# Feed-forward of a six-layer block: its input fetched by DMA, its first products in three passes of a rounded format

## The chip, the cores and the metric

The kernel runs on one core of a Trainium2 chip. The core has a matrix engine (TensorE, PE in the rows; its weight loads are PEld), a vector engine (DVE), a scalar engine (ACT), GpSimd (POOL) and a queue that issues DMAs (SP). They run their own instruction lists and wait for each other on semaphores. The metric is the device time of one execution in microseconds; lower is better.

## The reference

The input `x` is 16 sequences of 128 tokens of 128 features. It goes through four stages, each added to `x`: a 16-head cross attention, a mixture of 16 experts, a latent cross attention with rotation, and then the stage that takes most of the time, six layers of

```
for i in range(DEPTH):                     # DEPTH = 6
    x = attn_layer(shift_tokens(x), Wqkv[i], ...) + x
    x = ffn_layer(shift_tokens(x), ln_g[i], ln_b[i], W1[i], b1[i], W2[i], b2[i]) + x

def shift_tokens(t):                       # second half of the features comes from the token before
    a, s = jnp.split(t, 2, -1)
    s = jnp.pad(s, ((0, 0), (1, 0), (0, 0)))[:, :-1]
    return jnp.concatenate([a, s], -1)

def ffn_layer(x, g, bln, W1, b1, W2, b2):
    xn = layer_norm(x) * g + bln
    a, gate = jnp.split(xn @ W1 + b1, 2, -1)   # W1 is 128 x 682
    return a * gelu(gate) @ W2 + b2            # W2 is 341 x 128
```

`attn_layer` is a windowed attention of 16 heads of 64. All is float32.

## The kernel before

Tokens stand on the 128 partitions. `Y` [128, 16, 128] holds the state of the six layers, one 128x128 tile for each of 16 sequences (b).

**Attention.** A sequence has four units of work (four heads each), so a layer has 64 units. Each engine runs a `Pipeline`: in slot c it does its steps for unit c minus the step's skew. So in one slot PE does, in this order, `l_scores` (unit c-5), `l_turn_qk` (c-4), `l_pv` (c-6), the projections (c-1), `l_output` (c-7), `l_turn_o` (c-6), `l_turn` (c-5) and `l_turn_x` (c). DVE does `l_peaks` (c-5), `l_sum_squares` (c-2), `l_divide` (c-6), `l_floor`, `l_residual`, `l_rotate` (c-1). POOL does `l_norm` (c-4: four small instructions, lines 541 to 548), `l_add` (c-3, line 534) and `l_scale` (c-4, line 555). The last slots of a layer, 64 to 70, are written `att.finish(0)` to `att.finish(6)`; in them only the units that are left are served. Note the skews: POOL's `l_add` of unit 63 needs only DVE's `l_rotate` of slot 64.

`l_pv` of the units of a sequence reads copies of the values in `stash` (`l_v2`, `l_v3`), which SP's queue makes by DMA: `move_values(b, q)` issues four DMAs of 65 KB once the values are there, and `l_pv` of unit 4b waits for all four of (b, 0). SP also fetches the shifted attention input of each sequence into `xin` with two DMAs (lines 367 and 368), of 128 rows and, for the shifted half of the features, of 127 rows.

**Feed-forward.** It runs in four groups g of four sequences, each with three chunks k of the hidden width (128, 128, 85). For a group: `f_shift` (PE, lines 923 and 924: two float32 products with an identity and a shifted identity put the shifted input into PSUM), `f_stats` (DVE, lines 1653 and 1658), the reciprocal root (POOL, lines 566 and 568), `f_norm` (DVE, line 1666), `f_turn` (PE, line 932: four transposes), `f_copy_n` (ACT, line 1227, to `f_nT`), then for each chunk `f_hidden` (PE, lines 948 and 949: two float32 products of 512 columns, each printed as two matmuls), `f_gelu` (ACT), `f_gated` (DVE), and `f_out` (PE, line 959) and `f_residual` (DVE). `f_hidden` of chunk i waits for `f_gated` of chunk i-2 (the banks alternate).

The first part is woven into the last slots: `into_feed_forward` puts steps between `att.finish(...)` calls, in an order written out by hand for each engine. The rest is in `out_of_feed_forward`, which also starts the next layer's attention and splits its weights (ACT `high_weights`, DVE `low_weights`). The attention's projections already use the format that the change brings to `f_hidden`: the operands are rounded to F32R ("high"), the remainder is kept as a second F32R tensor ("low"), and three passes high·high, high·low, low·high are added up in PSUM (lines 818 and 827).

## Time and profile before

| | us |
|---|---|
| median of 3 runs | 2300.74 (2296.83 to 2302.52) |
| the profiled execution, device time | 2298.88 |
| its span | 2297.1 |
| PE busy | 2163.7 (94%) |
| DVE busy | 1708.3 (74%) |
| ACT busy | 1555.0 (68%) |
| POOL busy | 1410.4 (61%) |
| chain that ended last: PE's share | 74% |

The profile is of one execution. The span runs from the first to the last instruction; the device time holds 1.8 us more. The six layers fill the stretch from about 560 us to the end, 288.6 us each.

### The profile page before, as it was taken

The page shows a single profiled execution, that of the slowest core. Times are in us where ns is not written, and L with a number is a line of the kernel's source. Part 1 is how long each engine was busy: PE and PEld are TensorE (multiplying, and loading weights), DVE is VectorE, ACT ScalarE, POOL GpSimd, SP SyncE. Part 2 cuts the span into 40 slices and gives each one's busy share as a digit, 9 for nine tenths or more (in the row PEclk, how much of TensorE's full clock was granted, in tenths as well). Part 3 has the DMA queues.
Part 4 walks back from the last instruction along what each step waited for, and adds up shares of the span by engine and source line. Part 5 has one row for each costly group of instructions (what it writes and reads, how often), then busy time and mean ns, then how long its engine had stood idle before and what let it go on. Part 6 is the DMA issues. An engine that isn't in the chain of part 4 may idle for free.

```text
span 2297.1 us, 104869 instructions
## 1 busy us (share of the span) xinstructions
PE 2163.7 (94%) x36357; PEld 1677.6 (73%) x36357; DVE 1708.3 (74%) x4617; ACT 1555.0 (68%) x5192; POOL 1410.4 (61%) x2639
## 2 busy tenths in 40 slices
PE   6999789998999989999899998999989999899998
PEld 4776267776888758887588875788857888578885
DVE  4777878886888758787578875778757877578874
ACT  3553545554888748887488884888848888478883
POOL 3442711112888728887288882888828888288881
PEclk9997999997999999999999999999999999999999
DMA  3000000001211102111021110311103111021110
GB/s 102 0 0 1 0 1 0 0 0 54 75 41 42 35 26 75 40 42 35 23 77 42 41 36 18 81 42 39 39 18 79 42 40 40 16 51 43 42 40 20
DMA packets 120016, 82.33 MB, mean 36 GB/s; under 512 B 50998, under 2 KB 112580, under 8 KB 119876
## 3 DMA queue, kind: packets, MB, share of 16 engines
q1 hardware_dynamic: 119876, 80.43, 13.5%
q8 instruction: 92, 1.51, 0.3%
q14 instruction: 48, 0.39, 0.1%
HBM read 21.94 MB, written 1.05 MB: 10 GB/s over the span
## 4 chain that ended last, share of the span: by engine, by line
PE 74%; issue 5%; DVE 4%; POOL 2%; ACT 1%; DVEq 0%; POOLq 0%; ACTq 0%
PE bank L818 14%; PE bank L835 9%; PE bank L902 7%; PE bank L882 6%; PE bank L862 6%; PE bank L827 6%; PE bank L892 4%; PE bank L845 4%; PE bank L757 2%; PE bank L854 2%; PE bank L746 2%; PE bank L949 2%; PE bank L948 2%; PE bank L605 2%; PE bank L959 1%
## 5 line engine op out<-in xcount | busy, mean ns | idle before, releaser
L534 POOL TENSOR_TENSOR l_qk<-l_rot 128x512 f32<-128x512 f32 x384 | 494.2, 1287 | 106.0 <-DVE l_rot L1597 58.8
L1593 DVE TENSOR_TENSOR l_rot<-bank,l_tab 128x512 f32<-128x512 f32 x384 | 265.0, 690 | 185.7 <-ACT l_sq L1194 185.1
L1210 ACT ACTIVATE l_qkT<-bank 128x512 f32<-128x512 f32 x384 | 229.6, 598 | 255.2 <-PE bank L835 255.2
L555 POOL TENSOR_TENSOR l_qk<-l_qk,l_rn 128x512 f32<-128x512 f32 x384 | 400.7, 1044 | 0.9
L1174 ACT ACTIVATE prob<-bank,peak 128x64 f32<-128x64 f32 x1536 | 353.9, 321 | 1.3 <-DVE peak L1615 1.3
L818 PE MATMUL bank<-w_high,xs_part 128*128 128x512 f32 x768 | 347.4, 452 | 6.0 <-DVE xs_part L1584 5.4
L1597 DVE TENSOR_TENSOR l_rot<-bank,l_tab 128x512 f32<-128x512 f32 x384 | 261.4, 681 | 0.0
L1607 DVE TENSOR_REDUCE l_ss<-l_sq 128x8 f32<-128x512 f32 x384 | 259.6, 676 | 0.2
L835 PE MATMUL bank<-const,l_qk 128*128 128x128 f32 x1536 | 252.9, 287 | 6.5 <-POOL l_qk L555 5.8
L1194 ACT ACTIVATE l_sq<-bank 128x512 f32<-128x512 f32 x384 | 236.0, 615 | 23.8 <-PE bank L818 16.0
L902 PE MATMUL bank<-l_wo,l_oT 128*128 128x128 f32 x1536 | 237.4, 277 | 0.0
L827 PE MATMUL bank<-w_high,xs_part 128*128 128x256 f32 x768 | 199.9, 283 | 11.6 <-issue 11.6
L902 PEld LDWEIGHTS bank<-l_wo,l_oT 128*128 128x128 f32 x1536 | 204.8, 191 | 3.3 <-issue 0.3
L835 PEld LDWEIGHTS bank<-const,l_qk 128*128 128x128 f32 x1536 | 161.9, 141 | 42.9 <-POOL l_qk L555 9.6
L818 PEld LDWEIGHTS bank<-w_high,xs_part 128*128 128x128 f32 x768 | 144.9, 189 | 63.9 <-DVE xs_part L1584 7.1
L882 PE MATMUL bank<-l_v,probT 64*32 64x65 f32 x4608 | 177.2, 223 | 10.0 <-ACT probT L1182 6.5
L439 POOL TENSOR_SCALAR ln_rs<-ln_mv 128x1 f32<-128x1 f32 (+1 forms) x64 | 14.5, 227 | 274.2 <-DVE ln_mv L1561 129.4
L1615 DVE TENSOR_REDUCE peak<-bank 128x4 f32<-128x256 f32 x384 | 160.0, 417 | 28.9 <-PE bank L862 27.3
L862 PE MATMUL bank<-l_qkT 64*32 64x64 f32 x12288 | 174.7, 222 | 0.0
L882 PEld LDWEIGHTS bank<-l_v,probT 64*32 64x32 f32 x4608 | 115.4, 106 | 79.1 <-issue 79.1
L1632 DVE TENSOR_TENSOR o<-bank,rsum 128x256 f32<-128x256 f32 x384 | 163.0, 424 | 13.3
L882 PE MATMUL bank<-stash,probT 64*32 64x65 f32 x7680 | 172.2, 223 | 0.0
(201 smaller groups left out, 5287.8 us busy)
## 6 DMA issues: line engine op xcount, KB each, us to landing
stash<-l_v SPq DMA_DIRECT2D x768, 65.0 KB, 2.0
early<-in_L_ffn_Wqkv_dram SPq DMA_DIRECT2D x36, 256.0 KB, 3.1
l_wo<-in_L_ffn_Wo_dram SPq DMA_DIRECT2D x6, 512.0 KB, 4.0
xin<-Y SPq DMA_DIRECT2D x96, 32.0 KB
xin<-Y SPq DMA_DIRECT2D x96, 31.8 KB
f_w<-in_L_ffn_W_dram SPq DMA_DIRECT2D x6, 341.0 KB
out_dram<-X SPq DMA_DIRECT2D x4, 256.0 KB, 2.3
f_w<-in_L_ffn_W_dram SPq DMA_DIRECT2D x6, 128.0 KB
```

The lines of the kernel that those rows point to most:

```text
L534: pool.tensor_tensor(l_qk[:, k], l_rot[:, k, 0], l_rot[:, k, 1], ALU.add).then_inc(l["add_done"], 1)
L555: pool.tensor_tensor(v, v, l_rn[:, k, :, None].broadcast_to([128, 8, L_DIM]), ALU.mult).then_inc(l["qk_done"], 1)
L818: ins = pe.matmul(bank[:, 0, :].rearrange("p (q n) -> p q n", q=2), xs_part[:, part, j // 4], w[:, 0:2, 256 * g:256 * g + 256], start=n == ...
L827: ins = pe.matmul(bank[:, 1, 0:256], xs_part[:, part, j // 4], w[:, 2, 256 * g:256 * g + 256], start=n == 0, stop=n == 2)
L835: ins = pe.transpose(bank[:, 2, n * 128:(n + 1) * 128], l_qk[:, j % 2, n * 128:(n + 1) * 128], ident)
L862: ins = pe.matmul(bank[w * WINDOW:(w + 1) * WINDOW, 3 + r, BAND * p:BAND * (p + 1)], l_qkT[rows, j % 2, queries:queries + WINDOW], l_qkT[r ...
L882: ins = pe.matmul(bank[w * WINDOW:(w + 1) * WINDOW, 6 - p, at:at + L_DIM + 1], probT[rows, j % 2, 128 * r + w * WINDOW:128 * r + (w + 1) * ...
L902: ins = pe.matmul(bank[:, 7, 256:384], l_oT[:, j // 4, p], l_wo[:, p], start=p == 0, stop=p == 7, skip_group_check=True)
L1174: ins = act.activation(prob[:, k, n * BAND:(n + 1) * BAND], bank[:, 3 + r, p * BAND:(p + 1) * BAND], ACT.Exp, bias=peak[:, k, n:n + 1])
L1593: dve.tensor_tensor(l_rot[:, k, 0].rearrange("p (q h n) -> p q h n", q=2, h=4), bank[:, 0, :].rearrange("p (q h n) -> p q h n", q=2, h=4), ...
L1597: dve.tensor_tensor(l_rot[:, k, 1].rearrange("p (q h s n) -> p q h s n", q=2, h=4, s=2), bank[:, 0, :].rearrange("p (q h s n) -> p q h s n ...
L1607: dve.tensor_reduce(l_ss[:, k, :, 0], l_sq[:].rearrange("p (h n) -> p h n", n=L_DIM), AX.X, ALU.add)\
```

## The change

Three things change in the six layers.

1. The shifted input of the feed-forward no longer comes from PE. SP copies it from `Y` to `f_x` (the memory of `m_xT`, free by then) with `take_feed_forward`: three groups at once behind the loop of `move_values`, when twelve sequences have their residual, and the last group when all have. DVE's statistics and normalisation read `f_x`, after a wait on the new semaphores `ld_fx`, and so does POOL before it adds `f_b2` to `Y`. `f_shift` is gone, and row 0 of the shifted half is set to zero once by POOL.
2. `f_hidden` does three F32R passes for each of its two products. For that ACT rounds `f_w1` to `f_wh` and each group's `f_nT` to `f_high`, and DVE makes the remainders `f_wl` and `f_low`.
3. Statistics, roots, normalisation and transposes are placed earlier and two groups apart, so `f_n`, `f_mv` and `f_rs` are doubled and the transposes alternate between banks 1 and 2.

The diff, cut; of the three `into_feed_forward` in it the first is POOL's, the second PE's, the third DVE's, and the `out_of_feed_forward` is DVE's.

```
+            def take_feed_forward(ly, first, end):
+                sp.wait_ge(l["res_done"], upto(ly * B, end))
+                apart(sp)
+                for b in range(first, end, 4):
+                    four = slice(b, b + 4)
+                    sp.dma_start(f_x[:, four, 0:HALF], Y[:, four, 0:HALF]).then_inc(ld_fx[b // 12], 16)
+                    sp.dma_start(f_x[1:, four, HALF:], Y[0:S - 1, four, HALF:]).then_inc(ld_fx[b // 12], 16)
...
+                take_feed_forward(ly, 0, 12)
                 for b in range(B - 2, B):
                     for q in range(2):
                         move_values(ly, b, b % 2, q)
+                take_feed_forward(ly, 12, 16)
...
+            pool.memset(f_x[0:1, :, HALF:], 0.0).then_inc(preset, 1)
...
             def into_feed_forward(ly, att):
+                rstd_n, bias = feed_forward(ly)
                 att.steady()
-                att.finish(0, 1, 2, 3)
+                att.finish(0)
+                rstd_n(0)
+                att.finish(1)
+                rstd_n(1)
+                att.finish(2, 3)
                 pool.wait_ge(ld_fw, (ly + 1) * (16 * FW_DMAS))
-                feed_forward(ly, 0)
+                bias(0)
...
-                    pe.matmul(bank[0:n, at, :], f_w1[:, FF + c0:FF + c0 + n], f_nT[:, g % 2], start=True, stop=True)
-                    pe.matmul(bank[0:n, at + 1, :], f_w1[:, c0:c0 + n], f_nT[:, g % 2], start=True, stop=True)\
-                      .then_inc(f["hidden"], 1)
+                    passes = (f_wh, f_high[:, g % 2]), (f_wl, f_high[:, g % 2]), (f_wh, f_low[g % 2])
+                    for half, first in ((0, FF + c0), (1, c0)):
+                        for m, (w, x) in enumerate(passes):
+                            ins = pe.matmul(bank[0:n, at + half, :], w[:, first:first + n], x, start=m == 0,
+                                            stop=m == 2)
+                    ins.then_inc(f["hidden"], 1)
...
             def into_feed_forward(ly, att):
-                att.finish(0, 1)
-                shift(0)
-                att.finish(2, 3)
+                att.finish(0, 1, 2)
+                turn_n(0)
+                att.finish(3)
+                turn_n(1)
                 pe.wait_ge(ld_fw, (ly + 1) * (16 * FW_DMAS))
-                turn_n(0)
                 att.finish(4)
                 hidden(0, 0)
-                att.finish(5)
-                shift(1)
-                att.finish(6)
+                att.finish(5, 6)
                 hidden(0, 1)
...
+                    act.activation(f_high[:, g % 2], f_nT[:, g % 2], ACT.Copy).then_inc(f["high_done"], 1)
...
+                act.activation(f_wh, f_w1[:], ACT.Copy).then_inc(f["wh_done"], 1)
...
             def into_feed_forward(ly, att):
-                att.finish(0, 1)
+                att.finish(0)
                 stats(0)
-                att.finish(2, 3)
+                att.finish(1)
+                stats(1)
                 norm(0)
+                att.finish(2)
+                norm(1)
+                dve.wait_ge(f["wh_done"], upto(0, ly + 1))
+                dve.tensor_tensor(f_wl, f_w1[:], f_wh.bitcast(F32), ALU.subtract).then_inc(f["w_split"], 1)
+                att.finish(3)
+                split(0)
                 att.finish(4, 5)
-                dve.wait_ge(ld_fw, (ly + 1) * (16 * FW_DMAS))
+                split(1)
                 gated(0, 0)
-                stats(1)
                 att.finish(6)
-                norm(1)
...
             def out_of_feed_forward(ly, nxt):
-                    if 0 < g < 3:
-                        stats(g + 1)
+                    if g < 2:
+                        stats(g + 2)
                     if g > 0:
                         gated(g, 0)
                     if 0 < g < 3:
-                        norm(g + 1)
+                        split(g + 1)
+                    if g < 2:
+                        norm(g + 2)
```

POOL, the last slots of the first layer, the kernel before: after the loop's branch come slot 64 (`finish(0)`: units 60, 61, 60) and slot 65. The row on `l_rn` ends `l_norm`, `l_qk<-l_rot` is `l_add`, `l_qk<-l_qk,l_rn` is `l_scale`.

```order
L73 COMPARE_AND_BRANCH
L541 TENSOR_TENSOR l_t<-l_s,l_y 128x8 [waits l_guessed]
L543 TENSOR_TENSOR l_t<-l_t,l_y 128x8 [waits l_newton]
L546 TENSOR_SCALAR l_t<-l_t 128x8 [waits l_newton]
L548 TENSOR_TENSOR l_rn<-l_t,l_y 128x8 [waits l_newton]
L534 TENSOR_TENSOR l_qk<-l_rot 128x512 [waits l_qk_turned,l_rot_done]
L555 TENSOR_TENSOR l_qk<-l_qk,l_rn 128x512 [waits l_rn_done,l_add_done]
L541 TENSOR_TENSOR l_t<-l_s,l_y 128x8 [waits l_guessed]
L543 TENSOR_TENSOR l_t<-l_t,l_y 128x8 [waits l_newton]
L546 TENSOR_SCALAR l_t<-l_t 128x8 [waits l_newton]
L548 TENSOR_TENSOR l_rn<-l_t,l_y 128x8 [waits l_newton]
```

The changed kernel at the same place:

```order
L73 COMPARE_AND_BRANCH
L576 TENSOR_TENSOR l_t<-l_s,l_y 128x8 [waits l_guessed]
L578 TENSOR_TENSOR l_t<-l_t,l_y 128x8 [waits l_newton]
L581 TENSOR_SCALAR l_t<-l_t 128x8 [waits l_newton]
L583 TENSOR_TENSOR l_rn<-l_t,l_y 128x8 [waits l_newton]
L569 TENSOR_TENSOR l_qk<-l_rot 128x512 [waits l_qk_turned,l_rot_done]
L590 TENSOR_TENSOR l_qk<-l_qk,l_rn 128x512 [waits l_rn_done,l_add_done]
L602 TENSOR_SCALAR f_rs<-f_mv 128x4 [waits f_stat]
L604 TENSOR_TENSOR f_rs<-f_rs,minus_half 128x4 [waits f_pool_st]
L576 TENSOR_TENSOR l_t<-l_s,l_y 128x8 [waits l_guessed]
L578 TENSOR_TENSOR l_t<-l_t,l_y 128x8 [waits l_newton]
L581 TENSOR_SCALAR l_t<-l_t 128x8 [waits l_newton]
```

The two instructions on `f_rs`, which wait for DVE's `f_stat`, now stand between the scale of unit 60 and the work on unit 61, and once more behind slot 65; before, they stood behind all of the attention's work.

DVE at the same place, the changed kernel (L1640 and L1644 are `l_rotate` of unit 63, the last of slot 64; L1677 and L1679 are `l_divide` of unit 59):

```order
L1640 TENSOR_TENSOR l_rot<-bank,l_tab 128x512 [waits l_sq_done,l_add_done]
L1644 TENSOR_TENSOR l_rot<-bank,l_tab 128x512
L1700 BN_STATS f_st<-m_xT 128x6 [waits ld_fx0]
L1700 BN_STATS f_st<-m_xT 128x6 x3
L1705 BN_AGGR f_mv<-f_st 128x2 [waits f_stats]
L1705 BN_AGGR f_mv<-f_st 128x2 x3
L1662 TENSOR_REDUCE peak<-bank 128x4 [waits l_exp_done,l_s_done]
L1654 TENSOR_REDUCE l_ss<-l_sq 128x8 [waits l_floored,l_sq_done]
L1677 RECIPROCAL rsum<-bank 128x4 [waits l_pv_done,l_o_turned]
L1679 TENSOR_TENSOR o<-bank,rsum 128x2x128 [waits l_rsum_done]
L1669 TENSOR_REDUCE l_s<-l_ss 128x8 [waits l_rn_done,l_ss_done]
L1700 BN_STATS f_st<-m_xT 128x6 [waits ld_fx0]
```

The statistics of group 0 follow slot 64 directly, and those of group 1 follow slot 65, whose `l_divide` waits for PE's `l_pv` of the same slot; before, `stats(0)` stood behind slot 65 and `stats(1)` behind slot 69.

SP's queue behind the loop, the changed kernel (`m_xT` is the memory of `f_x`; the `stash` rows are `move_values` of sequences 14 and 15):

```order
L404 DMA m_xT<-Y 128x4x64 [waits l_res_done]
L405 DMA m_xT<-Y 127x4x64
L404 DMA m_xT<-Y 128x4x64
L405 DMA m_xT<-Y 127x4x64
L404 DMA m_xT<-Y 128x4x64
L405 DMA m_xT<-Y 127x4x64
L383 DMA stash<-l_v 64x260 [waits l_v_done,l_pv_done]
L383 DMA stash<-l_v 64x260 x3
```

The six copies to `f_x`, three of them with 127 rows, stand ahead of the copies of values that `l_pv` of units 56 to 63 waits for; before, the `stash` rows followed each other.

## Rows read from the trace of the kernel before

**Rows 1.** The page, busy time of each engine and its share of the span.
```profile
PE 2163.7 (94%) x36357; PEld 1677.6 (73%) x36357; DVE 1708.3 (74%) x4617; ACT 1555.0 (68%) x5192; POOL 1410.4 (61%) x2639
```

**Rows 2.** Groups by shape: count, then busy us, mean ns, idle before, releaser.
```profile
L1676 DVE SCALAR_TENSOR_TENSOR f_h<-bank,f_b,f_ge 128x512 f32<-128x512 f32 x48 | 35.6, 741 | 5.5 <-ACT f_ge L1235 5.5
...
L1235 ACT ACTIVATE f_ge<-bank,f_b 128x512 f32<-128x512 f32 x48 | 33.0, 687 | 95.7 <-PE bank L949 95.7
...
L1745 DVE TENSOR_TENSOR w_low<-early,w_high 128x512 fp32r<-128x512 f32 x36 | 23.0, 680 | 1.2 <-ACT w_high L1278 1.2
...
L1278 ACT ACTIVATE w_high<-early 128x512 fp32r<-128x512 f32 x36 | 20.5, 616 | 0.0
```

**Rows 3.** PE in time, first layer's feed-forward: start us, us, line, [idle before].
```profile
811.35 1.02 PE L948 MATMUL bank<-f_nT,f_w 128*128 128x512 f32 x2
...
815.74 0.65 PE L932 MATMUL bank<-const,f_n 128*128 128x128 f32 x4 [2.51 <-DVE f_n L1666]
...
817.95 0.60 PE L923 MATMUL bank<-Y,const 128*128 128x256 f32 x2
...
818.81 1.02 PE L948 MATMUL bank<-f_nT,f_w 128*128 128x512 f32 x2
...
820.53 2.84 PE L959 MATMUL bank<-f_w,f_h 128*128 128x128 f32 x24
...
840.45 0.40 PE L818 MATMUL bank<-w_low,xs_part 128*128 128x512 f32 x1
840.68 0.40 PE L818 MATMUL bank<-w_high,xs_part 128*128 128x512 f32 x1
...
841.27 2.84 PE L959 MATMUL bank<-f_w,f_h 128*128 128x128 f32 x24
```

**Rows 4.** PE in time, just before that.
```profile
780.10 0.66 PE L835 MATMUL bank<-const,l_qk 128*128 128x128 f32 x4
...
790.89 0.66 PE L835 MATMUL bank<-const,l_qk 128*128 128x128 f32 x4
...
794.80 0.44 PE L835 MATMUL bank<-const,l_qk 128*128 128x128 f32 x2
```

**Rows 5.** POOL in time, same stretch.
```profile
785.79 1.06 POOL L555 TENSOR_TENSOR l_qk<-l_qk,l_rn 128x512 f32<-128x512 f32 x1
786.84 0.20 POOL L541 TENSOR_TENSOR l_t<-l_s,l_y 128x8 f32<-128x8 f32 x1
...
789.34 1.05 POOL L555 TENSOR_TENSOR l_qk<-l_qk,l_rn 128x512 f32<-128x512 f32 x1
...
812.85 0.23 POOL L566 TENSOR_SCALAR f_rs<-f_mv 128x4 f32<-128x4 f32 x1 [13.90 <-DVE f_mv L1658]
813.17 1.04 POOL L568 TENSOR_TENSOR f_rs<-f_rs,minus_half 128x4 f32<-128x4 f32 x1
```

**Rows 6.** DVE in time, same stretch.
```profile
790.60 0.68 DVE L1597 TENSOR_TENSOR l_rot<-bank,l_tab 128x512 f32<-128x512 f32 x1
...
792.35 0.42 DVE L1632 TENSOR_TENSOR o<-bank,rsum 128x256 f32<-128x256 f32 x1
...
794.53 0.89 DVE L1653 BATCH_NORM_STATS2 f_st<-bank 128x6 f32<-128x128 f32 x4 [1.68 <-PE bank L924]
```

**Rows 7.** SP's queue in time: start and length of issuing.
```profile
761.41 2.41 SPq L360 DMA_DIRECT2D stash<-l_v  x4
...
768.73 1.76 SPq L360 DMA_DIRECT2D stash<-l_v  x3
```

**Rows 8.** DMA from 825 to 832 us, 40 slices, and one issue.
```profile
GB/s 0 0 0 0 0 0 0 0 0 0 0 0 129 59 0 0 15 18 18 113 18 59 141 19 25 23 18 18 19 18 18 19 18 19 18 18 19 7 0 0
...
xin<-Y SPq DMA_DIRECT2D x2, 31.8 KB
```

**Rows 9.** PE in time, second layer's feed-forward.
```profile
1104.81 1.92 PE L949 MATMUL bank<-f_nT,f_w 128*85 128x512 f32 x2
```

**Rows 10.** DVE in time, start of the cross-attention of the latents.
```profile
288.44 0.34 DVE L1518 TENSOR_SCALAR nx<-early,ln_mv,ln_rs 128x128 f32<-128x128 f32 x1 [5.02 <-POOL ln_rs L441]
```

More of the change, by code:

```diff
@@ L94, in sb, with over @@
             return ctx.enter_context(nc.sbuf_tensor(name, shape, dt))
+        def over(name, shape, at, first=0):
+            return nc.alloc_sbuf_tensor_at(name, shape, F32R, offset=at + 4 * first)
         def sem(name):
@@ L227, in build @@
         f_st = sb("f_st", [128, 4, 6])
-        f_mv = sb("f_mv", [128, 4, 2])
-        f_rs = sb("f_rs", [128, 4])
-        f_n = sb("f_n", [128, 4, D])
+        f_mv = sb("f_mv", [128, 2, 4, 2])
+        f_rs = sb("f_rs", [128, 2, 4])
+        f_n0 = sb("f_n", [128, 4, D])
+        f_n = (f_n0[:], c_oT[:, 1])
+        f_wh, f_wl = over("f_wh", [128, 2 * FF], at_c_v)[:], over("f_wl", [128, 2 * FF], at_c_v, 704)[:]
+        f_high = over("f_high", [128, 2, 512], at_sm)
+        f_low = over("f_low0", [128, 512], at_c_k)[:], over("f_low1", [128, 512], at_xcT)[:]
+        f_x = m_xT[:]
         f_nT = sb("f_nT", [128, 2, 512])
@@ L244, in build @@
         ld_xin = [sem(f"ld_xin{k}") for k in range(2)]
+        ld_fx = [sem(f"ld_fx{k}") for k in range(2)]
         tables, scaled_q = sem("tables"), sem("scaled_q")
@@ L269, in build @@
                  "add_done qk_done qk_turned qkT_done v_done o_turned oT_done out_done res_done")
-        f = stage_sems("f_", "xs stats stat pool_st rstd n_done turned nT_done hidden gelu_done h_done out_mm yb_done "
+        f = stage_sems("f_", "wh_done w_split high_done split stats stat pool_st rstd n_done turned nT_done hidden gelu_done h_done out_mm yb_done "
                  "y_done")
@@ L278, in apart, with feed_forward_read @@
             eng.sem_inc(passed[eng.engine], 1)
+        def feed_forward_read(eng, ly, g):
+            late = g // 3
+            eng.wait_ge(ld_fx[late], (ly + 1) * (32 if late else 96))
         def one(t3, b):
@@ L1257, in out_of_feed_forward @@
                         gelu(g, 0)
+                    if 0 < g < 3:
+                        copy_n(g + 1)
+                    if g > 0:
                         gelu(g, 1)
@@ L1506, in c_stats @@
                     dve.bn_stats(ln_st[:, 0], one(X, b))
-                    dve.bn_stats(ln_st[:, 1], one(CTX, b)).then_inc(c["stats"], 1)
-                    dve.wait_ge(c["stats"], upto(0, b + 1))
+                    dve.bn_stats(ln_st[:, 1], one(CTX, b)).then_inc(ln["stats"], 1)
+                    dve.wait_ge(ln["stats"], upto(B, b + 1))
                     apart(dve)
                     dve.bn_aggr(ln_mv[:, 0], ln_st[:, 0])
-                    dve.bn_aggr(ln_mv[:, 1], ln_st[:, 1]).then_inc(c["ln_stat"], 1)
+                    dve.bn_aggr(ln_mv[:, 1], ln_st[:, 1]).then_inc(ln["stat"], 1)
             def c_norm(u, b, j):
@@ L1648, in f_stats @@
                 def f_stats(g):
-                    dve.wait_ge(f["xs"], upto(0, fb + g + 1))
-                    v = bank[:, 1, :].rearrange("p (a n) -> p a n", a=4)
+                    feed_forward_read(dve, ly, g)
+                    v = f_x[:, 4 * g:4 * g + 4]
                     apart(dve)
```

113 lines of the change are left out of this document (62 added, 51 removed).

## The prediction, made before the changed kernel ran

> **What bounds the kernel now.** I read the page first: PE is busy for 94% of the span, the next engine for 74% [rows 1]. So a microsecond that PE waits is a microsecond of the kernel, and the other engines matter where PE waits for them. Then I read PE in time through the feed-forward of one layer. Three kinds of row are to be seen in [rows 3]. The old input step costs from 817.95 to 818.81, 0.86 us for its two products. A hidden chunk in float32 costs from 818.81 to 820.53, 1.72 us. And before the transposes of group 1 PE waits 2.51 us for DVE. The rounded format is in the same rows: two F32R passes of 512 columns start 0.23 us apart (840.45, 840.68). In the last slots of the attention PE runs one slot in 3.6 us, read from the transposes of q and k; those of unit 58 start at 780.10 and of unit 61 at 790.89 [rows 4]. I call P the moment at which PE has finished all attention and starts the second hidden chunk: 811.35 [rows 3].
>
> Then the two queues that the change reorders, POOL [rows 5] and SP [rows 7]. POOL runs ahead of PE: it ends the scale of unit 60 at 786.84 and that of unit 61 at 790.38, half a microsecond before PE turns the latter [rows 4, 5]. There is no slack of a slot here, only of half a microsecond. SP is idle between its copies of values: (13, 1) is issued by 763.82, (14, 0) starts at 768.73 [rows 7].
>
> **What the change takes away.** Per layer four input steps, 4 x 0.86 = 3.4 us of PE. Twelve hidden chunks become six passes of 0.23 us, 1.4 us each with no wait, against 1.72: 12 x 0.3 = 3.7 us. The wait of 2.51 us is not wholly gone. The transposes of group 2 take the place of those of group 1, after two chunks instead of one (P + 2.8). They need the last residual, the statistics of group 2, the root and the normalisation in a row. The statistics take 0.89 us and four small aggregations, together 1.3 [rows 6]; the root comes 1.4 us after POOL starts, with semaphores 1.6 [rows 5]; four normalisations take 1.3. That is P + 4.6 or so, and leaves a wait of 1.9 us.
>
> From there I walked the list of each engine, with gelu 0.69 us, gate 0.74, remainders and weight splits 0.68 and 0.62 [rows 2]. DVE then has about 8 us of work for a group that takes PE 7.5, and the gate of chunk i-2 holds PE back by a few tenths per group. If the input is always there in time, the product behind group 2 starts at P + 23.8 where it starts now at 841.27, P + 29.9. With two shorter chunks behind it the feed-forward after P is **6.7 us shorter**.
>
> **What it adds on SP, first.** The six copies to `f_x` are issued from 764.2 on, ahead of the values of sequence 14. A copy of the shifted half has 127 rows. In the trace two such copies of 31.8 KB run from slice 16 to 36 of [rows 8], 20 slices of 0.175 us = 3.5 us, at 18 GB/s, while the 128-row copies appear as peaks of 59 to 141 GB/s. So the 127-row copies don't spread over the DMA engines, and two of them run one behind the other. The new ones are four times as large: 130 KB / 18 GB/s = 7.1 us each, 21.3 for three, and with the start (1.2 us behind the issue in the same rows) and the shares of the normal copies the last is through at about 788.5. The shape of four blocks per row is not in the trace; if it spread over four engines, the three would be done in some 5 us. I take the long end, since the row count is what both shapes share.
>
> The Trainium skill (DMA: Bandwidth & Descriptors, "Why a DMA increments its semaphore by 16 and not by 1") says that the number of engines is the largest number up to 16 that divides the slowest dimension of both sides, that 127 partitions give one, and that it is then the lowest-numbered engine. By that rule the new shape is on one engine as well; the trace shows this for the small copies (18 GB/s), and no row shows it for the large.
>
> The copies of (14, 0) go out at 768.73 as before, but a part of each lies on the engine that is taken, behind the long copies. They land at about 789.9. PE needs them for the products of unit 56, behind the transposes of unit 58, that is at 780.7 [rows 4]. **PE waits 9.2 us** once per layer, and as all engines serve the same slots, all of them shift.
>
> The last group's input is copied when all residuals are there, P + 0.3. Its shifted copy of 7.1 us lands at P + 10.5. DVE reaches those statistics at P + 7.3 and stands until then, with the gates of group 1 behind them in its queue. In the walk this costs PE 3.2 us, so the gain after P is **3.5 us** and not 6.7.
>
> **What it adds on POOL.** The root of group 0 now stands before the work on unit 61. It waits for DVE's statistics, and these stand behind the rotation of unit 63, which ends at 791.2 [rows 6]. So it can't start before 791.2 + 1.3 + 0.2 = 792.8, and ends at 794.2, while POOL was free at 786.84 [rows 5]. Norm, add and scale of unit 61 take from 786.84 to 790.38 now, 3.54 us; they end at 797.7. PE turns unit 61 at 797.75 instead of 790.89: 6.9 us late. The second root does it again. DVE's statistics of group 1 stand behind the division of unit 59, and this needs products that PE does behind that turn. From turn to division end is 1.9 us now (790.89 to 792.77, [rows 4, 6]), so the statistics run from 799.7 to 801.1, the root ends at 802.65, and unit 62 is scaled at 806.2. PE turns it at 806.2 instead of 794.80 [rows 4]: **11.4 us late**. What follows up to P I take as even: the two input steps that fall away (1.7) against ACT's two extra roundings of 0.6 us ahead of copies that PE waits for, [rows 2], and DVE's extra work.
>
> **The clock.** After the wait of 2.5 us the second layer's product of group 0 took 1.92 us [rows 9] where 1.02 is usual [rows 3]: TensorE was granted its lower level, 1.2 GHz, for some microseconds. Such stretches cost 0 to 1.7 us in each layer now, 1.45 on average. In the changed kernel PE stands 9, 6.8 and 5.5 us in a layer. The work behind each runs at half speed at first; I put 1.5 us to each, 4.5 in all, **3.0 more** than now.
>
> **Sum.** Per layer 9.2 + 11.4 - 3.5 + 3.0 = 20.1 us, six times 120.6. Once, the zeroing of row 0 on POOL lies ahead of the first root of the latent attention, for which DVE waits 5.02 us already [rows 10]: between nothing and 3 us, I take 1.5. 122 us on the profiled execution of 2298.9 give 2421; the median is 1.9 higher, so **2423 us**.
>
> **Rivals.**
> A. The shifted copies spread and nothing waits for them. For it: no row has this shape. Then per layer 11.4 - 6.7 + 1.5 (clock) = 6.2, in all 37 + 1.5: 2339 us.
> B. The copies delay as I say, but the POOL order is harmless, because the skew of POOL's list differs from my reading. Against it: scale of 61 ends 0.5 us ahead of PE's turn of 61. Then 9.2 - 3.5 + 1.5 + 0.3 = 7.5 per layer, 2347 us.
> C. The passes don't come at 0.23 us but at the pace of float32, since each changes its weights; [rows 3] speak against it, those passes change theirs too. Then 3.7 us per layer more: 2445 us.
> D. Faster: PE's shorter feed-forward decides. It does if both waits together cost less than the 6.7 us per layer that are saved, that is if the copies have landed by 782 and the roots find their statistics done. Then about 6.4 us less per layer: 2264 us. The list of POOL speaks against it: DVE can't have the statistics before 792.6, whatever the copies do.
>
> **Chances.** My forecast 0.70, A 0.12, B 0.07, C 0.06, D 0.05. Within the forecast the landing time (1 us either way), the clock (2 us) and what is even before P (2 us) give 6 x 3 = 18 us either way, 2400 to 2445. 0.8 needs A or B as well, so the range is 2335 to 2445. A difference of 0.3% is what a measurement of this kernel can tell from none: faster 0.05, same 0.01, slower 0.94.
>
> **What would show it.** In the changed kernel's trace: PE's products of unit 56 with a wait of some 9 us on the copies, once per layer; a stretch of 20 us at 18 GB/s before it; POOL's root instruction with 5.8 us of idle time ahead, released by DVE's statistics, and again with 3 us; PE's turns of units 61 and 62 waiting 6.8 and 5.5 us for POOL. Hidden chunks 1.4 us apart. I am wrong if the first is missing (A), if the second is (B), if chunks take 1.7 us (C), or if neither wait shows (D).

## The result and the profile after

The changed kernel takes 2452.66 us (median of 4 runs, 2451.03 to 2454.5), the kernel before 2299.35; the ratio is 1.0663, 95% interval 1.0645 to 1.0681. I had forecast 2423 with a range up to 2445: the direction was right, and the loss is 153 us where I had worked out 122. The profiled span is 2449.9 us.

The page of the changed kernel, engines ([rows 1] before), and the two longest waits of PE over the whole span (total us, times, longest):

```profile
PE 2168.1 (88%) x36405; PEld 1721.6 (70%) x36405; DVE 1742.6 (71%) x4647; ACT 1571.9 (64%) x5222; POOL 1413.2 (58%) x2640
...
PE bank L885 <- POOL l_qk L590: 71.1, 15, 6.6
PE bank L932 <- DMA stash<-l_v: 61.5, 6, 10.3
```

PE stands for 281.8 us (span less busy) where it stood for 133.4. The two rows are the two waits that the prediction named, the transposes of q and k for POOL (5.8 us in all before) and the products for the copied values (none before). Together they are 127 of the 148 us. But PE's busy time is the other half of the reading: the change takes work off PE, and yet PE is busy for 4.4 us longer. Some of the same matmuls run at half speed.

PE in the first layer, the waits ([rows 4] and [rows 3] before; P is now at 835.40, 24.05 us later than 811.35):

```profile
790.90 0.28 PE L932 MATMUL bank<-l_v,probT 64*32 64x65 f32 x1 [10.34 <-DMA stash<-l_v]
...
809.18 1.12 PE L885 MATMUL bank<-const,l_qk 128*128 128x128 f32 x4 [6.56 <-POOL l_qk L590]
...
818.15 1.11 PE L885 MATMUL bank<-const,l_qk 128*128 128x128 f32 x4 [4.41 <-POOL l_qk L590]
...
841.08 0.66 PE L972 MATMUL bank<-const,f_n 128*128 128x128 f32 x4 [2.62 <-DVE f_n L1713]
...
852.55 0.66 PE L972 MATMUL bank<-const,c_oT 128*128 128x128 f32 x4 [2.08 <-DVE c_oT L1713]
```

The four transposes of unit 61 take 1.12 us and took 0.66 in [rows 4]. They ran in the lower level of the clock (granted 0.50 from 809.18 to 810.30). SP's queue at the same place ([rows 7] before), start and length of issuing:

```profile
764.03 0.70 SPq L404 DMA_DIRECT2D m_xT<-Y  x1
764.78 0.80 SPq L405 DMA_DIRECT2D m_xT<-Y  x1
765.62 6.44 SPq L404 DMA_DIRECT2D m_xT<-Y  x1
772.11 0.70 SPq L405 DMA_DIRECT2D m_xT<-Y  x1
772.85 6.87 SPq L404 DMA_DIRECT2D m_xT<-Y  x1
779.76 0.69 SPq L405 DMA_DIRECT2D m_xT<-Y  x1
780.78 16.09 SPq L383 DMA_DIRECT2D stash<-l_v  x12
```

The copies don't only land late: the next one can't be issued. The issue of a 128-row copy (L404) takes 6.44 and 6.87 us behind a 127-row copy (L405), 0.70 otherwise. So the values of sequence 14 go out at 780.78; the working had them go out at 768.73.

POOL, its two roots with the wait ahead and the scale (L590) of units 61 and 62 behind them ([rows 5] before), then DVE's statistics and normalisations ([rows 6]; the last three rows belong to groups 2 and 3):

```profile
804.42 0.23 POOL L602 TENSOR_SCALAR f_rs<-f_mv 128x4 f32<-128x4 f32 x1 [5.93 <-DVE f_mv L1705]
...
808.08 1.04 POOL L590 TENSOR_TENSOR l_qk<-l_qk,l_rn 128x512 f32<-128x512 f32 x1
813.30 0.33 POOL L602 TENSOR_SCALAR f_rs<-f_mv 128x4 f32<-128x4 f32 x1 [4.18 <-DVE f_mv L1705]
...
817.06 1.04 POOL L590 TENSOR_TENSOR l_qk<-l_qk,l_rn 128x512 f32<-128x512 f32 x1
```

```profile
802.84 0.86 DVE L1700 BATCH_NORM_STATS2 f_st<-m_xT 128x6 f32<-128x128 f32 x4
...
839.06 1.96 DVE L1713 TENSOR_SCALAR f_n<-m_xT,f_mv,f_rs 128x128 f32<-128x128 f32 x4 [1.68 <-POOL f_rs L604]
...
846.45 0.87 DVE L1700 BATCH_NORM_STATS2 f_st<-m_xT 128x6 f32<-128x128 f32 x4 [2.92 <-DMA m_xT<-Y]
...
849.53 2.96 DVE L1713 TENSOR_SCALAR c_oT<-m_xT,f_mv,f_rs 128x128 f32<-128x128 f32 x4 [0.42 <-POOL f_rs L604]
```

The rows of POOL and the first of DVE are the order that the prediction told of: idle times of 5.93 and 4.18 us ahead of the roots, where it gave 5.8 and 3. The late copy is there too (2.92). What it did not have is the length of four normalisations, 1.96 and 2.96 us: before, four took 1.36 us.

### The profile page after: what moved, and what is told of

The parts are those of the page before. It is cut to its first block, busy times and chain, and to the rows that moved or that the text cites. A ratio compares the mean times of both kernels' runs of the same rounds, so it can differ in the third digit from the quotient of the medians.

```text
span 2449.9 us, 105121 instructions
## 1 busy us (share of the span) xinstructions
PE 2168.1 (88%) x36405; PEld 1721.6 (70%) x36405; DVE 1742.6 (71%) x4647; ACT 1571.9 (64%) x5222; POOL 1413.2 (58%) x2640
## 4 chain that ended last, share of the span: by engine, by line
PE 66%; SPq 7%; issue 5%; POOL 3%; DVE 3%; DMA 3%; ACT 2%; POOLq 0%; DVEq 0%; ACTq 0%
PE bank L868 12%; PE bank L885 8%; PE bank L952 6%; PE bank L932 6%; PE bank L877 5%; PE bank L912 5%; SPq L404 4%; PE bank L942 3%; PE bank L895 3%; SPq L383 2%; DMA m_xT<-Y 2%; PE bank L992 2%; PE bank L807 2%; PE bank L1003 2%; PE bank L904 2%
## 5 line engine op out<-in xcount | busy, mean ns | idle before, releaser
L590 POOL TENSOR_TENSOR l_qk<-l_qk,l_rn 128x512 f32<-128x512 f32 x384 | 400.7, 1044 | 0.9
L1640 DVE TENSOR_TENSOR l_rot<-bank,l_tab 128x512 f32<-128x512 f32 x384 | 265.3, 691 | 182.2 <-ACT l_sq L1234 181.3
L885 PE MATMUL bank<-const,l_qk 128*128 128x128 f32 x1536 | 258.8, 292 | 71.5 <-POOL l_qk L590 71.1
L1644 DVE TENSOR_TENSOR l_rot<-bank,l_tab 128x512 f32<-128x512 f32 x384 | 261.5, 681 | 0.0
L952 PE MATMUL bank<-l_wo,l_oT 128*128 128x128 f32 x1536 | 245.5, 284 | 2.8 <-ACT l_oT L1256 2.8
L952 PEld LDWEIGHTS bank<-l_wo,l_oT 128*128 128x128 f32 x1536 | 210.8, 197 | 8.0 <-ACT l_oT L1256 4.3
L877 PE MATMUL bank<-w_high,xs_part 128*128 128x256 f32 x768 | 201.4, 284 | 11.5 <-issue 11.5
L1677 DVE RECIPROCAL rsum<-bank 128x4 f32<-128x4 f32 x384 | 68.9, 179 | 172.1 <-PE bank L932 171.1
L1679 DVE TENSOR_TENSOR o<-bank,rsum 128x256 f32<-128x256 f32 x384 | 163.0, 425 | 13.3
```

Source lines behind the costliest of these rows:

```text
L590: pool.tensor_tensor(v, v, l_rn[:, k, :, None].broadcast_to([128, 8, L_DIM]), ALU.mult).then_inc(l["qk_done"], 1)
L877: ins = pe.matmul(bank[:, 1, 0:256], xs_part[:, part, j // 4], w[:, 2, 256 * g:256 * g + 256], start=n == 0, stop=n == 2)
L885: ins = pe.transpose(bank[:, 2, n * 128:(n + 1) * 128], l_qk[:, j % 2, n * 128:(n + 1) * 128], ident)
L952: ins = pe.matmul(bank[:, 7, 256:384], l_oT[:, j // 4, p], l_wo[:, p], start=p == 0, stop=p == 7, skip_group_check=True)
L1640: dve.tensor_tensor(l_rot[:, k, 0].rearrange("p (q h n) -> p q h n", q=2, h=4), bank[:, 0, :].rearrange("p (q h n) -> p q h n", q=2, h=4), ...
L1644: dve.tensor_tensor(l_rot[:, k, 1].rearrange("p (q h s n) -> p q h s n", q=2, h=4, s=2), bank[:, 0, :].rearrange("p (q h s n) -> p q h s n ...
```

## The experiments

All ratios are against runs of the kernel before on the same chip. None of these kernels leaves out a part of the computation.

**e1_rows_b, the copies.** One edit of the changed kernel:

```
-  sp.dma_start(f_x[1:, four, HALF:], Y[0:S - 1, four, HALF:])
+  sp.dma_start(f_x[1:113, four, HALF:], Y[0:112, four, HALF:])
+  sp.dma_start(f_x[113:, four, HALF:], Y[112:S - 1, four, HALF:])
```

> The changed kernel with one edit: each shifted copy of 127 rows is made as two, of 112 and of 15 rows. Theory (copies on one engine hold back the values): PE's wait of 10.3 us per layer for the stash copies goes, with the slow-clock work behind it 11.7 us per layer, and the last group's input is in time, worth another 0 to 3 us; the waits for POOL stay. 6 x 11.7 to 6 x 14.7: 2365 to 2383 us. Rival (it is the number of copies ahead in SP's queue, or their bytes, and not the row count): the wait stays at 8 us or more and the time at 2435 to 2453 us.

2363.41 us, ratio 1.027 (1.0246 to 1.0295): 89 us less than the changed kernel, 14.9 per layer, 2 us better than the best of the theory. The wait for `stash` is gone from PE's list. The GB/s of the DMA from 764 to 800 us, 40 slices, first the changed kernel, then this one:

```profile
GB/s 81 100 55 15 18 18 18 18 18 78 95 18 18 18 18 18 18 18 155 18 18 18 18 18 18 18 55 121 88 95 116 82 66 0 0 103 118 75 0 0
```

```profile
GB/s 78 74 145 128 17 159 119 67 173 62 74 83 131 8 0 119 103 74 0 0 0 0 0 82 131 83 0 18 0 0 0 0 132 90 74 0 0 0 0 0
```

Three plateaus at 18 GB/s, of 5 to 7 slices of 0.9 us, become one burst of some 12 slices. The long copies were issued 7.3 and 7.7 us apart (764.78, 772.11, 779.76), so I put one at about 7.5 us rather than the 7.1 of the working.
**e8_dose, the same cause in part.** Only the first group's copy is split.

> The changed kernel with the shifted copy of the first group alone split into 112 and 15 rows; those of groups 1, 2 and 3 stay at 127 rows. Theory (each 127-row copy occupies one engine for 7.1 us, one behind the other, and the values wait for the sum): PE's wait for the stash copies is 10.3 - 7.1 = 3.2 us per layer, the late input of group 3 stays, and so do the waits for POOL: 2453 - 6 x (7.1 to 8) = 2405 to 2410 us. Rival (the wait comes from SP's queue, whose issuing is blocked as long as any such copy is behind another): the wait stays at 7 us or more, or is gone with one copy less: 2435 us or more, or 2390 us or less.

2423.99 us, ratio 1.0536 (1.0521 to 1.0551): 29 us less, 4.8 per layer instead of 7.1, so 14 us above the 2405 to 2410 of the theory, and in neither range of the rival. PE's wait and SP's queue:

```profile
PE bank L936 <- DMA stash<-l_v: 30.5, 6, 5.2
```

```profile
768.47 0.78 SPq L409 DMA_DIRECT2D m_xT<-Y  x1
769.29 6.46 SPq L404 DMA_DIRECT2D m_xT<-Y  x1
775.78 0.69 SPq L409 DMA_DIRECT2D m_xT<-Y  x1
776.80 23.23 SPq L383 DMA_DIRECT2D stash<-l_v  x13
```

The wait halves, from 10.3 to 5.2 us, though I had said 3.2. The first long copy is issued at 768.47 here and at 764.78 in the changed kernel, 3.7 us later; PE comes to its wait 1.1 us later as well (781.71 against 780.56). One copy of 7.5 us less and a start that is 2.6 us later make 10.3 - 7.5 + 2.6 = 5.4. So the sum over one engine holds within 0.2 us, and I had missed that splitting one copy also moves the others. By this arithmetic the block at issue adds nothing, since the values' share on that engine would have stood behind the same copies. No run takes the block away alone.

**e2_order_b, the order on POOL.** The roots behind slot 67, DVE's and PE's steps moved with them:

```
  POOL                          DVE                        PE
- att.finish(0)                 - norm(0) after finish(1)  - turn_n(0) after finish(2)
- rstd_n(0)                     - norm(1) after finish(2)  - turn_n(1) after finish(3)
- att.finish(1)                 + norm(0), norm(1)         + turn_n(0), turn_n(1)
- rstd_n(1)                     +   after finish(3)        +   after finish(3)
- att.finish(2, 3)
+ att.finish(0, 1, 2, 3)
+ rstd_n(0)
+ rstd_n(1)
```

> The changed kernel with the order of the hand-written part put back to the old principle: POOL does the roots of groups 0 and 1 behind slot 67, DVE normalises them behind its slot 67, PE transposes them behind its slot 67; the copies stay. Theory (the roots ahead of units 61 and 62 hold POOL, and PE with it): PE's waits for the scale of units 61 and 62 (6.6 and 4.4 us in the first layer, 11.9 us per layer over all) go, and the wait for the copies of 10.3 us stays: 2453 - 6 x 11.9 = 2382 us, some 10 us less if the slow clock behind these waits goes with them. Rival (PE would have had to wait there anyway, for DVE or ACT, which the late copies push back): 2425 to 2453 us.

2391.82 us, ratio 1.0395 (1.037 to 1.0421): 61 us less, 10.1 per layer, 10 us short of what I expected. PE's wait for POOL falls from 71.1 to 4.5 us. But its waits for DVE's normalisation rise from 19.0 to 31.6 us and those for DVE's `o` from 5.5 to 13.3, which is in the main why less than 11.9 per layer came back: the order put back has waits of its own.

**e3_both_b, both.**

> Both edits at once. Theory: neither wait is left, and what remains is what the change does behind the attention. If that is the 6.7 us per layer of my walk, 2299 - 40 = 2259 us. Rival (DVE's normalisation now reads SBUF and is slowed beside POOL, 1.1 us to 2.0 and 3.0 us, which holds the hidden chunks back): only 1 to 3 us per layer are left, 2281 to 2293 us.

2301.31 us, ratio 1.0004 (0.999 to 1.0017). No difference from the kernel before can be measured. The parts add up: 89 + 61 + 2 = 152 of the 153 us. Neither of my two expectations held; the gain behind the attention, which the prediction put at 6.7 us per layer, is not small here but absent from the total. This is the step to settle. The total hides two things, which the table further down gives for all six layers: behind P 20 us are gained, not 40, and ahead of P 22 us are lost. That loss isn't one of the changed kernel: e3 has neither the order of before nor that of the change.

**e4_passes_b, the passes alone.** The kernel before with `f_hidden` as in the change; the input still comes from `f_shift` in the old order.

```
  ACT                          DVE                       PE
  att.finish(0)                att.finish(2)             f_hidden:
+ f_wh <- f_w1               + f_wl <- f_w1 - f_wh       - 2 products, float32
...                            att.finish(4)             + 2 x 3 passes, F32R
  f_nT <- bank               + split(0)
+ f_high <- f_nT             ...
                               gated(g, 1)
                             + split(g + 1)
                               gated(g, 2)
```

> The kernel before with the second part of the change alone: f_hidden in three F32R passes, the input still made by PE, the old order of all steps. Theory (a pass starts 0.23 us after the one before, a chunk costs 1.4 instead of 1.72 us and the roundings are covered): 12 x 0.3 = 3.7 us per layer, 2299 - 22 = 2277 us. Rival (rounding on ACT and remainder on DVE, 1.2 us and a wait each, stand between the copy of the transposes and the next group's first chunk, and PE has only one chunk and an input step to cover them): the gain is eaten, 2295 to 2310 us.

2299.78 us, ratio 1.0 (0.9987 to 1.0013). Again nothing. PE is busy for 15.7 us less (2148.0) and stands for 15.3 longer. Three rows of its waits make it up, first this kernel, then the kernel before:

```profile
PE bank L963 <- DVE f_n L1705: 26.6, 20, 2.8
...
PE bank L913 <- ACT probT L1217: 11.1, 10, 1.8
...
PE bank L983 <- DVE f_low L1711: 6.4, 10, 1.0
```

```profile
PE bank L932 <- DVE f_n L1666: 22.1, 18, 2.5
...
PE bank L882 <- ACT probT L1182: 6.5, 6, 1.1
```

44.1 against 28.6 us: PE, faster, waits for the normalisation that did not become faster, and ACT's roundings stand ahead of copies that PE needs. My rival for this run (2295 to 2310 us) came out.

**e5_bias, the collision of POOL and DVE.** The kernel of e3, and POOL waits with its additions of `f_b2` until DVE has normalised:

```
+ pool.wait_ge(f["n_done"], upto(0, ly * 4 + 2))
  bias(0)
...
  rstd_n(2)
+ pool.wait_ge(f["n_done"], upto(0, ly * 4 + 3))
  bias(1)
  rstd_n(3)
+ pool.wait_ge(f["n_done"], upto(0, ly * 4 + 4))
  bias(2)
```

> The kernel with split copies and the old principle of order, and POOL's additions of f_b2 to Y moved: each waits until DVE has normalised the group that it would otherwise run beside. Theory (POOL's float32 additions slow DVE's instructions that read and write SBUF): the normalisations of groups 0, 2 and 3, 2.2, 2.0 and 2.1 us in the first layer, take 1.1 us each, and the remainder 0.68 us instead of 1.48; PE's waits for f_n shrink by some 1 us twice per layer and the slow clock behind them in part: 2301 - 6 x (1 to 3) = 2283 to 2295 us. Rival (they are slow because of POOL's roots, or for a reason of their own): durations as before, 2298 to 2304 us.

2272.96 us, ratio 0.9884 (0.9869 to 0.9898): 28 us less than e3, for additions that start a little later, and 10 us better than the best that I had expected. In e3 they stand beside each other, POOL in time, then DVE (first layer, group 0; then the two shapes of the normalisation over the whole span, duration in ns min/median/max):

```profile
799.58 1.04 POOL L605 TENSOR_TENSOR f_rs<-f_rs,minus_half 128x4 f32<-128x4 f32 x1
800.59 1.27 POOL L610 TENSOR_TENSOR Y<-Y,f_b 128x512 f32<-128x512 f32 x1
```

```profile
800.50 2.21 DVE L1710 TENSOR_SCALAR f_n<-m_xT,f_mv,f_rs 128x128 f32<-128x128 f32 x4
802.63 1.10 DVE L1710 TENSOR_SCALAR c_oT<-m_xT,f_mv,f_rs 128x128 f32<-128x128 f32 x4
```

```profile
L1710 DVE TENSOR_SCALAR f_n<-m_xT,f_mv,f_rs x48: 329/334/1439, 800.5 to 2266.2; 128x128 f32<-128x128 f32 x48
L1710 DVE TENSOR_SCALAR c_oT<-m_xT,f_mv,f_rs x48: 332/335/1329, 802.6 to 2274.2; 128x128 f32<-128x128 f32 x48
```

The first of these two shapes in e5, then the normalisation in the kernel before:

```profile
L1713 DVE TENSOR_SCALAR f_n<-m_xT,f_mv,f_rs x48: 336/343/352, 800.6 to 2236.6; 128x128 f32<-128x128 f32 x48
```

```profile
L1666 DVE TENSOR_SCALAR f_n<-bank,f_mv,f_rs x96: 396/402/411, 799.9 to 2277.0; 128x128 f32<-128x128 f32 x96
```

The median of e3 is as in e5; the longest is four times as long. So it is not that all run slower: single instructions are held until POOL's addition is over, and the rest run at full speed. The kernel before normalised out of PSUM, and none of its 96 took longer than 411 ns, though 72 of them ran beside the same additions of POOL; so with group 1:

```profile
814.18 1.26 POOL L571 TENSOR_TENSOR Y<-Y,f_b 128x512 f32<-128x512 f32 x1
```

```profile
814.24 1.36 DVE L1666 TENSOR_SCALAR f_n<-bank,f_mv,f_rs 128x128 f32<-128x128 f32 x4 [1.42 <-POOL f_rs L568]
```

Who starts first matters. In e3, second layer, the normalisation that starts 0.22 us before POOL's addition takes 0.34 us, the next one, 0.03 us behind its start, 1.32. (The second row of DVE holds both.) The recorded start isn't quite the moment that counts: in the first layer (rows above) the first normalisation starts 0.09 us before the addition, at 800.50, and is held all the same, for 1.44 us.

```profile
1089.43 0.34 DVE L1710 TENSOR_SCALAR f_n<-m_xT,f_mv,f_rs 128x128 f32<-128x128 f32 x1
```

```profile
1089.43 1.57 DVE L1710 TENSOR_SCALAR f_n<-m_xT,f_mv,f_rs 128x128 f32<-128x128 f32 x2
```

```profile
1089.65 1.27 POOL L610 TENSOR_TENSOR Y<-Y,f_b 128x512 f32<-128x512 f32 x1
```

The Trainium skill (SBUF — State Buffer, "Who interferes with whom") states this as an exclusive lock on a port pair that VectorE and GpSimd share, held for a whole instruction, for VectorE's faster modes; an instruction with two SBUF inputs, it says, contends with what GpSimd reads. The traces agree, with 1.1 us for one holding. By the change's third part the normalisation moved into that conflict, and the diff shows it only as another source tensor.

**e11_after_bias, the same edit in the changed kernel.**

> The changed kernel with POOL's additions of f_b2 moved behind the normalisations, as in e5, and nothing else. Theory (the price of DVE and POOL in each other's way behind the attention adds to the two waits): the normalisations of groups 2 and 3 take 1.1 us instead of 2.0 and 3.0; as the late copy of the last group's input stays, some of it is covered: 2453 - 6 x (1.5 to 4.7) = 2425 to 2444 us. Rival (with PE held up by the copies and by POOL anyway, that collision costs nothing here): 2448 to 2456 us.

2435.5 us, ratio 1.0591 (1.0575 to 1.0607): 17 us less, 2.9 per layer. So the collision costs beside the two large waits too, and I had it nowhere in the sum. Of the 17 us, 14.5 lie behind P (the table below).

**e6_turns, e9_act, e10_round, the order once more.** On e5, three steps. e6 moves the transposes to where no engine is hurried; PE's part of it:

```
  att.finish(0, 1, 2, 3)          for g in range(4):
  turn_n(0)                     -     if 0 < g < 3:
- turn_n(1)                     -         turn_n(g + 1)
  att.finish(4)                       if g > 0:
  hidden(0, 0)                            hidden(g, 0)
  att.finish(5)                           output(g - 1)
+ turn_n(1)                     +         turn_n(g + 1)    # g < 3
  att.finish(6)                           hidden(g, 1)
```

DVE's `norm(1)` stands behind `finish(4)`, `norm(g + 2)` behind `gated(g, 2)`, and its remainders (`split`) move with them; ACT's `copy_n(1)` stands behind `gelu(0, 0)`. e9 is e6 with

```
  ACT                       DVE
  gelu(0, 0)                  att.finish(4)
- copy_n(1)                 - norm(1)
  att.finish(6)               split(0)
+ copy_n(1)                 + norm(1)
                              att.finish(5)
                              gated(0, 0)
                            - split(1)
                              att.finish(6)
                            + split(1)
```

and e10 parts ACT's rounding from its copy:

```
  copy_n(0)
- f_high <- f_nT
  att.finish(4)
+ f_high <- f_nT
  att.finish(5)
```

> The last kernel, and the transposes of a group placed where no engine has to hurry: those of group 1 behind hidden(0,0) and slot 69, those of groups 2 and 3 behind the product of the group two before, DVE's normalisation behind the last gate of a group. Theory (what ate the gain behind the attention is the wait of PE for f_n and the slow clock after it, two to three times per layer): both go, from P to the product behind group 2 it is 22 us instead of 26.8, and before P 2 us are saved: 2301 - 6 x (5 to 8) = 2253 to 2271 us. Rival (DVE, or ACT with its additional roundings, bounds a group at about 8 us, whatever the order): 2285 us or more.

> The kernel of e6 with two moves: ACT copies and rounds group 1 behind its last attention step (slot 70) instead of ahead of it, and DVE makes the remainder of group 0 before it normalises group 1 and that of group 1 behind slot 70. Theory (the last slots of the attention are a chain through PE, DVE and ACT, and what stands on ACT ahead of its copies of that chain delays it): PE's wait of 1.8 us per layer for the last copy l_oT and its wait for f_low go, with the slow clock behind them; P falls by 2 to 3 us per layer: 2290 - 6 x (2 to 3.5) = 2269 to 2278 us. Rival (it is the clock, which stays low there for reasons that this doesn't touch): 2285 to 2292 us.

> The kernel of e9, and ACT rounds group 0 to f_high behind slot 68 instead of ahead of it. Theory (the same chain): the products of unit 62, which wait 1.7 us for the copy of probT, start 0.6 us earlier, and so does all behind them: another 6 x 0.6 = 4 us off e9. Rival (the remainder of group 0 then comes late for hidden(0,0)): nothing, or 3 us longer than e9.

e6: 2290.11 us, ratio 0.9952 (0.9939 to 0.9965). e9: 2266.3, 0.9855 (0.9838 to 0.9872). e10: 2257.59, 0.9814 (0.9801 to 0.9827). For e6 my expectation (2253 to 2271) was missed: it is 17 us slower than e5, from which it is made. The time is that of its rival (2285 or more), but not for the rival's reason, a bound "whatever the order", since e9 changes only the order. e9 and e10 came out 3 and 5 us better than theirs. In the table, a is the stretch from PE's transposes of `o` in slot 67 to P, b from P to the product behind group 2, both of the first layer. "Ahead" runs from PE's transposes of q and k of unit 58 to P, "behind" from P to the product behind group 3, both summed over the six layers. All in us:

| kernel | median | PE busy | PE not busy | a | b | ahead | behind |
|---|---|---|---|---|---|---|---|
| before | 2299.35 | 2163.7 | 133.4 | 11.2 | 29.9 | 184.0 | 242.9 |
| after | 2452.66 | 2168.1 | 281.8 | 9.7 | 29.1 | 337.6 | 239.6 |
| e1 rows | 2363.41 | 2151.6 | 210.7 | 9.7 | 26.1 | 269.7 | 221.6 |
| e2 order | 2391.82 | 2158.1 | 231.2 | 13.7 | 29.1 | 276.4 | 238.2 |
| e3 both | 2301.31 | 2140.3 | 159.5 | 14.1 | 26.8 | 206.4 | 222.7 |
| e5 bias | 2272.96 | 2124.7 | 145.2 | 13.6 | 23.5 | 196.6 | 203.1 |
| e11 bias, after | 2435.5 | 2153.1 | 279.1 | 9.7 | 27.2 | 334.0 | 225.1 |
| e6 turns | 2290.11 | 2141.8 | 149.2 | 15.3 | 23.2 | 214.6 | 207.3 |
| e9 act | 2266.3 | 2123.0 | 142.9 | 11.3 | 22.6 | 189.1 | 205.5 |
| e10 round | 2257.59 | 2118.7 | 137.5 | 9.8 | 22.7 | 182.4 | 203.4 |

Behind P, e6 gains nothing over e5, and ahead of P it loses 18 us. In e6 ACT copies and rounds group 1 ahead of the last copy of the attention, and PE waits for that (first ACT, then PE):

```profile
813.68 0.78 ACT L1269 ACTIVATE f_nT<-bank,f_g 128x512 f32<-128x512 f32 x1 [2.05 <-PE bank L974]
814.49 0.63 ACT L1272 ACTIVATE f_high<-f_nT 128x512 fp32r<-128x512 f32 x1
815.02 0.37 ACT L1258 ACTIVATE l_oT<-bank 128x256 f32<-128x256 f32 x1
```

```profile
815.44 1.22 PE L954 MATMUL bank<-l_wo,l_oT 128*128 128x128 f32 x4 [1.80 <-ACT l_oT L1258]
```

Ahead of P PE's own work isn't the bound. The last units go through PE, DVE and ACT in turn, with little beside them; PE's steps in between mostly fill its waits. So I read it that two input steps less did not shorten a, and that 1.4 us of copying and rounding on ACT did lengthen it. e9 moves steps of ACT and of DVE at once, and its share of either wasn't measured apart; e10 moves one rounding of ACT alone and is 8.7 us faster for it. With these steps behind the chain, ahead of P is as short as in the kernel before (182.4 against 184.0), and e10 is 1.9% faster than that kernel.

**e12_bias_back.** e10 without the three lines `+ pool.wait_ge(f["n_done"], ...)` of e5.

> The kernel of e10 with POOL's additions of f_b2 back where they were: behind the roots, beside DVE's normalisations. It asks whether the collision of DVE and POOL costs as much where the normalisations of groups 2 and 3 aren't hurried. Theory (a held-up instruction costs only where the next engine waits for it): only group 0's, ahead of which PE stands in any case, reaches the path, 1.1 us and some slow clock, 2258 + 6 x (1.1 to 2) = 2264 to 2270 us. Rival (it costs whatever the order, as between e3 and e5): 28 us, 2286 us.

2271.5 us, ratio 0.9877 (0.9858 to 0.9896), just above the 2264 to 2270 of the theory: 14 us more than e10, where the same edit was worth 28 between e3 and e5. In the first layer b is 22.8 us, as in e10, and a 11.5 instead of 9.8. Over the six layers ahead of P is 192.1 us, 9.7 longer than in e10, and behind it 209.1, 5.7 longer. So most of the cost is at group 0, for which PE waits, as the theory had it, but the held-up instructions behind P aren't free either.

**e7_float32, the passes' own price.** On e6:

```
- passes = (f_wh, f_high[:, g % 2]), (f_wl, f_high[:, g % 2]), (f_wh, f_low[g % 2])
+ passes = ((f_w1[:], f_nT[:, g % 2]),)
```

> The last kernel with f_hidden in float32 as before the change: one product of f_w1 and f_nT for each half, the roundings and remainders still made but not read. It prices the three passes alone. Theory (1.4 against 1.72 us per chunk, all of it on the path once PE doesn't wait): 12 x 0.3 x 6 = 22 us longer than with the passes. Rival (the gates bound the chunks, PE waits a little more when it is faster): 0 to 8 us longer.

2308.3 us, ratio 1.0037 (1.0025 to 1.0049): 18.2 us more than e6, that is 0.25 us per chunk, a little less than the 0.3 us of the working. Both kernels make the roundings and remainders, so this is the price of the passes alone. What the roundings themselves cost isn't in it; in the order of e4 they took the whole gain.

**The clock.** The changed kernel and all that are made from it but e7 give PE the same 36405 matmuls. So a difference in PE's busy time is speed alone. Against e10 (2118.7, whose mean granted clock of 0.98 is that of the kernel before) the changed kernel has 49.4 us more, 8.2 per layer, at a mean of 0.944; e1 32.9, e2 39.4, e3 21.6, e6 23.1, e5 6.0. Behind the long waits the work runs at half speed, and behind some short ones: in e3 the six passes of `hidden(1,0)` start 0.43 us apart after the wait of 2.66 us for `f_n`, 0.23 elsewhere. In e5 the same wait is 1.81 us and the passes behind it come at 0.23.

## Why the prediction was right and wrong

The prediction's clock term of 3.0 us is for three stops; I give each a third. The stretches of the table above part the sum as the prediction did, since e1 takes away the copies and leaves the order:

| term, us in all | predicted | measured |
|---|---|---|
| ahead of P, copies: 9.2 + 1.0, six times | 61 | 68 (after less e1) |
| ahead of P, POOL's order: 11.4 + 2.0, six times | 80 | 86 (e1 less before) |
| behind P, with the input in time: -6.7, six times | -40 | -21 (e1 less before) |
| behind P, the late input: 3.2, six times | 19 | 18 (after less e1) |
| once, the zeroing on POOL | 1.5 | nothing: the first layer's first transposes of q and k start at 567.0 us, 567.4 before |
| elsewhere | | 2 |
| sum | 122 | 153 |

- **The copies** were right in mechanism and nearly in size. That 127 rows of the new shape don't spread was the open question of the working, and the long end was right (e1, e8). PE waits 10.3 us instead of 9.2. Rival A (the copies spread) is out.
- **POOL's order** was right, the waits too: 6.56 and 4.41 us against 6.8 and 5.5. e2 gives back only 61 of the 86 us, since the order that it puts in place is itself longer ahead of P than that of the kernel before, by 22 us (e3). Rival B is out, and with A and B rival D, as both waits are there.
- **The pace of the passes**: 0.23 us apart, as forecast (e7: 0.25 us gained per chunk). Rival C is out.
- **The step that failed is the gain behind P: 6.7 us per layer with the input in time, 3.5 with the late input.** Measured are 3.6 (e1) and 0.55 (the changed kernel). The walk put four normalisations at 1.3 us, with nothing in their way. From SBUF one of them can be held for the length of an addition on POOL, and behind P two groups' normalisations take 1.96 and 2.96 us. Without this collision the walk comes out: 3.0 us per layer in e11, which keeps the late input (forecast 3.5), and 6.6 in e5, which has it in time (forecast 6.7). It is 17 of the 31 us that were missing (e11). The range had room for the landing of the copies, the clock and what is even before P, and none for the gain behind it.
- **"What follows up to P I take as even"** held in the changed kernel: from the transposes of unit 62 to P it takes 104.6 us in six layers against 95.5, that is 1.5 us per layer more, what the prediction gives to the clock behind one stop. It does not hold in the order of e3, where this stretch takes 115.9, and moving ACT's and DVE's steps gives that back (92.0 in e10).
- **The clock** was put at 3.0 us more per layer; the changed kernel loses 8.2 per layer against e10. PE's time shows the miss from the other side: PE's idle time rose by 148 us, where my 9.2, 6.8 and 5.5 make 129, and the work saved, 43 us by the working, was all spent on the slower level. I had priced 1.5 us per stop and, in the changed kernel, no stop shorter than 5 us; the wait of 2.66 us in e3 has it too. By the stretches 12 us are missing ahead of P: some 6 of them are the longer wait for the copies, the rest was not parted further.

What e10 gains over the kernel before is the forecast gain: 39.5 us behind P and 1.6 ahead of it, together 41 of the 42 by which the medians differ. The first layer alone would mislead (a and b differ by 8.6 us, six times that is 52), because a is 11.2 us or more in only two of the six layers of the kernel before and 10.2 in the others. What stays open is which of the steps put between the last slots makes the order of e3 22 us longer ahead of P; only one rounding on ACT was moved by itself (e10).

## What to carry to other kernels

Where several engines hand one item on with little beside it, as in the last slots of a pipeline, ask of every step that is woven in on which engine it stands and what it stands ahead of, before you ask how long it is. When an operand moves from PSUM to SBUF, look for what GpSimd does at that moment: here this point was 17 of the 31 us that the forecast missed. When an experiment puts back an old order, check that the order is the old one, or its waits are booked to the wrong term. And count the stops: what the matmuls at half speed cost behind them here, 8.2 us per layer, is more than the 7.1 us of work that the change saved.
